# A routing step's list of tokens per slot: one-hot rows compared eight tiles at a time, the token number multiplied in on GpSimd

## The reference

```
x = x + layernorm(attention(layernorm(x)))        # 16 query heads, one key/value head, causal
x = x + layernorm(ffn(layernorm(x)))

def ffn(x):                                       # T = 4096 tokens
    probs = softmax(x @ router.T)                 # 8 experts
    top_v, top_i = top_k(probs, 2); top_v /= sum(top_v)
    out = sum over a token's two experts e of top_v * expert_e(x)      # 352 wide, silu-gated
    return out + sigmoid(x @ shared_gate.T) * shared_expert(x)          # 1408 wide, silu-gated
```

## Time and profile before

| | us |
|---|---|
| median of 3 runs | 2149.88 |
| lowest and highest of them | 2144.54, 2150.34 |
| the profiled execution, its own time | 2153.74 |
| its span, first to last instruction | 2152.0 |
| mean granted TensorE clock, share of full | 0.943 |
| PE busy, share of the span | 92% |
| DVE busy | 52% |
| ACT busy | 36% |
| POOL busy | 22% |

### The profile page before, as it was taken

How to read it: one execution, slowest core, us unless ns; L and a number is a source line. 1 busy time by engine, 2 the same in 40 slices (tenths; PEclk the granted TensorE clock), 3 DMA queues, 4 the chain that set the end, 5 groups by cost and what they waited for, 6 DMA issues and landing times. The chain is left out here.

```text
span 2152.0 us, 34973 instructions
## 1 busy us (share of the span) xinstructions
PE 1973.5 (92%) x11932; PEld 1568.8 (73%) x11932; DVE 1129.8 (52%) x2478; ACT 781.6 (36%) x1576; POOL 478.2 (22%) x1087
## 2 busy tenths in 40 slices
PE   5989999999999743899999999999999999999995
PEld 3665656656565422799999999978888888888884
DVE  4556656666565328677777657643433324333243
ACT  3445545455453410466666546432111111111111
POOL 1223324234241320211111112001113021130212
PEclk9799999999999765899999989999999999999998
DMA  5144353442533132566666657632123020230202
GB/s 173 51 114 127 117 174 106 147 143 109 176 98 126 50 113 95 195 237 236 235 235 235 240 188 268 243 113 69 37 81 118 19 97 31 86 117 19 97 24 94
DMA packets 114453, 281.47 MB, mean 131 GB/s; under 512 B 11680, under 2 KB 26272, under 8 KB 105024
## 3 DMA queue, kind: packets, MB, share of 16 engines
q1 hardware_dynamic: 103328, 244.18, 32.9%
q0 software_dynamic: 11040, 36.18, 5.0%
HBM read 198.79 MB, written 78.12 MB: 129 GB/s over the span
## 5 line engine op out<-in xcount | busy, mean ns | idle before, releaser
L1257 PE MATMUL ex_bank<-ex_xT,ex_gu 128*128 128x256 f32 (+12 forms) x2808 | 358.0, 284 | 1.0 <-DVE ex_xT L1421 1.0
L1257 PEld LDWEIGHTS ex_bank<-ex_xT,ex_gu 128*128 128x128 f32 (+1 forms) x2808 | 344.1, 185 | 4.9 <-issue 1.4
L1289 DVE TENSOR_TENSOR sh_silu<-sh_silu,sh_bank 128x512 f32<-128x512 f32 x88 | 60.6, 688 | 457.4 <-ACT sh_silu L1282 451.1
L1282 ACT ACTIVATE sh_silu<-sh_bank 128x512 f32<-128x512 f32 x88 | 52.6, 598 | 591.4 <-PE sh_bank L1257 546.1
L1257 PE MATMUL sh_bank<-sh_xT,sh_gate 128*128 128x512 f32 x1056 | 256.2, 392 | 5.2 <-DVE sh_dn L1704 5.2
L677 DVE TENSOR_REDUCE at_nmax<-at_bank 128x1 fp32r<-128x384 f32 (+3 forms) x512 | 222.6, 476 | 61.2 <-PE at_bank L438 60.7
L1269 PE MATMUL sh_bank<-sh_dn,sh_act 128*128 128x512 f32 x1056 | 254.3, 390 | 0.0
L1257 PE MATMUL sh_bank<-sh_xT,sh_up 128*128 128x512 f32 x1056 | 253.7, 389 | 0.0
L1257 PEld LDWEIGHTS sh_bank<-sh_xT,sh_gate 128*128 128x128 f32 x1056 | 199.8, 189 | 47.3 <-issue 5.6
L869 ACT ACTIVATE at_PT<-at_bank 128x512 f32<-128x512 f32 (+1 forms) x384 | 184.2, 506 | 125.7 <-PE at_bank L451 101.0
L1269 PEld LDWEIGHTS sh_bank<-sh_dn,sh_act 128*128 128x128 f32 x1056 | 197.6, 188 | 43.7 <-DVE sh_act L1298 2.9
(11 more groups left out here) (228 smaller groups left out, 2653.8 us busy)
## 6 DMA issues: line engine op xcount, KB each, us to landing
ex_gu_in<-gu_in SPq DMA_DIRECT2D x39, 1408.0 KB
at_Qs<-q_dram SPq DMA_DIRECT2D x96, 256.0 KB, 4.0
ex_dn_in<-dn_in SPq DMA_DIRECT2D x39, 512.0 KB
ys<-sh_yk SPq DMA_DIRECT2D x35, 512.0 KB, 2.9
q_dram<-at_q_h SPq DMA_DIRECT2D x64, 256.0 KB, 3.2
xnT<-at_xT SPq DMA_DIRECT2D x16, 1024.0 KB, 5.0
sh_xT<-xnT SPq DMA_DIRECT2D x16, 1024.0 KB
at_x_in<-x_in SPq DMA_DIRECT2D x8, 1024.0 KB, 5.1
```

The source lines that it names most:

```text
L1257: last = self.nc.tensor.matmul(self.gate_up_ps[c % 2][which][0:m, 0:w], cols(i, k), self.xT[j][:, k, 0:w], start=(step == 0), stop=(step = ...
L1282: nc.scalar.activation(silu[c % 2][0:m, 0:w], gate_up_ps[c % 2][0][0:m, 0:w], ACT.Silu).then_inc(s["silu_ready"], 1)
L1289: nc.vector.tensor_tensor(silu[c % 2][0:m, 0:w], silu[c % 2][0:m, 0:w], gate_up_ps[c % 2][1][0:m, 0:w], ALU.mult).then_inc(s["product"], 1)
```

## The change

The one-hot rows of lanes are made eight tiles at a time as well, by one tensor_tensor compare of 128x1024 elements, without the token's number. The number is multiplied into the columns' side instead, by a tensor_tensor of 128x592 on GpSimd, from `column_hot` into a new tile `column_token`, which is what PE reads. All three tiles now have two buffers, used in turn by the PARTS = 8 parts (m) of eight picks. DVE signals `column_ready` behind each column compare, GpSimd `token_ready` behind each product. PE waits once for each part, for both its sides, and signals `used` once for each part. DVE waits before the column compare of part m for the product of part m - 2, and before the lane compare for the matmuls of part m - 2; GpSimd waits for these too, before it writes `column_token`.

```diff
-        lane_hot = [sb(f"lane_hot{k}", [P, P], F32R) for k in range(4)]
-        column_hot = sb("column_hot", [P, 2, NTT, SC], F32R)
+        PART = NTT // 4
+        PARTS = 2 * NTT // PART
+        lane_hot = [sb(f"lane_hot{k}", [P, PART, P], F32R) for k in range(2)]
+        column_hot = [sb(f"column_hot{k}", [P, PART, SC]) for k in range(2)]
+        column_token = [sb(f"column_token{k}", [P, PART, SC], F32R) for k in range(2)]
...
         def _(pool):
...
+            for m in range(PARTS):
+                t = m * PART % NTT
+                pool.wait_ge(column_ready, m + 1)
+                if m >= 2:
+                    pool.wait_ge(used, m - 1)
+                nc.gpsimd.tensor_tensor(column_token[m % 2][:], column_hot[m % 2][:],
+                                        token_no[:, t:t + PART].unsqueeze(2).to_broadcast([P, PART, SC]),
+                                        ALU.mult).then_inc(token_ready, 1)
...
         def _(pe):
...
-            for n in range(2 * NTT):
-                pe.wait_ge(hot, n + 1)
-                last = nc.tensor.matmul(inverse_ps[:, 0:SC], lane_hot[n % 4][:],
-                                        column_hot[:, n // NTT, n % NTT, :],
-                                        start=(n == 0), stop=(n == 2 * NTT - 1))
+            for m in range(PARTS):
+                pe.wait_ge(hot, m + 1)
+                pe.wait_ge(token_ready, m + 1)
+                for t in range(PART):
+                    last = nc.tensor.matmul(inverse_ps[:, 0:SC], lane_hot[m % 2][:, t, :], column_token[m % 2][:, t, :],
+                                            start=(m == t == 0), stop=(m == PARTS - 1 and t == PART - 1))
                 last.then_inc(used, 1)
...
         def _(dve):
...
-            for n in range(2 * NTT):
-                k, t = divmod(n, NTT)
-                if t % PART == 0:
-                    nc.vector.tensor_tensor(column_hot[:, k, t:t + PART, :],
-                                            column_no[:].unsqueeze(1).to_broadcast([P, PART, SC]),
-                                            digit_f[:, 0, k, t:t + PART].unsqueeze(2).to_broadcast([P, PART, SC]),
-                                            ALU.is_equal)
-                if n >= 4:
-                    dve.wait_ge(used, n - 3)
-                nc.vector.tensor_scalar(lane_hot[n % 4][:], lane_no[:], digit_f[:, 1, k, t:t + 1],
-                                        token_no[:, t:t + 1], ALU.is_equal, ALU.mult).then_inc(hot, 1)
-            dve.wait_ge(used, 2 * NTT)
+            for m in range(PARTS):
+                k, t = divmod(m * PART, NTT)
+                if m >= 2:
+                    dve.wait_ge(token_ready, m - 1)
+                nc.vector.tensor_tensor(column_hot[m % 2][:], column_no[:].unsqueeze(1).to_broadcast([P, PART, SC]),
+                                        digit_f[:, 0, k, t:t + PART].unsqueeze(2).to_broadcast([P, PART, SC]),
+                                        ALU.is_equal).then_inc(column_ready, 1)
+                if m >= 2:
+                    dve.wait_ge(used, m - 1)
+                nc.vector.tensor_tensor(lane_hot[m % 2][:], lane_no[:].unsqueeze(1).to_broadcast([P, PART, P]),
+                                        digit_f[:, 1, k, t:t + PART].unsqueeze(2).to_broadcast([P, PART, P]),
+                                        ALU.is_equal).then_inc(hot, 1)
+            dve.wait_ge(used, PARTS)
```

More of the change, by code:

```diff
@@ L1068, in build_routing @@
         own, expert_ready = sem("own"), sem("expert_ready")
-        PART = NTT // 4
+        column_ready, token_ready = sem("column_ready"), sem("token_ready")
         block = ctx.enter_context(nc.Block())
```

## The result

The changed kernel takes 2156.16 us at the median of 20 runs (2148.6 to 2159.31), the kernel before 2149.93 us in 20 runs beside them (2140.05 to 2154.74). The ratio is 1.0024 with a 95% interval of 1.0013 to 1.0035: slower by 0.24%, with an interval that reaches a little past 0.3%. The prediction had 2154.6 us and 0.22%. Its mechanism holds line by line in the trace. Its main sum does not: it made the list 4.7 us longer, and the trace shows 2.1 us.

A forecast was written before the change was run, and what follows sets the result against it. DVE was taken to pace the list. Eight parts in turns at 3.13 us, 25.0 us, plus the last burst of 2.04 put the cast 4.7 us later: 2149.9 + 4.7 = 2154.6 us, range 2146 to 2161.

The forecast's parts named there:

- Its mechanism: In the list's loop, DVE compares with two SBUF inputs and POOL's product take turns instead of overlapping.
- Its main sum: List loop: 3.13 us a part in turns, 25.0 us for eight; with the last burst, the cast comes 4.7 us later.
- What bounds, and what passes through: DVE paces the 22.51 us list stretch; everything behind is a chain, so its gain or delay reaches the kernel's end.
- The turns: In the list's loop, DVE's compares and POOL's product on SBUF run one after the other, 3.13 us a part.
- rival (a): In the list's loop, turns do not apply or cost little: 1.83 us a part, 5.3 us earlier, 2144.6 us; chance 0.12.
- Rows 8 to 10: Trace pairs near 11, 1551 and 177 us where POOL and DVE tensor_tensors on SBUF took turns, in both directions.
- DVE's terms: In each list part: column compare 0.69 us of pace, lane compare 1.22 us, pace 1.14; about 0.06 less taking over.
- The product: POOL's 592-element multiply in each list part: 1.45 us alone, in turns say 1.36 us.
- Rival (b): POOL's product is slower for its repeated operand: 4.1 us on top, 8.8 in all, 2158.7 us; chance 0.20.
- PE's bursts: Eight matmuls per list part, 0.23 us apart, 2.04 us a burst; only the last lies on the path.

The follow-up runs named there:

- experiments 2 and 8: Changed kernel with DVE's constant lane and column numbers read from PSUM, run twice: ratio to the kernel before 0.9979 both times, medians 2145.97 and 2145.6 us.
- experiment 2: Changed kernel with DVE's compares reading the constant lane and column numbers from PSUM, first run: 2145.97 us, ratio 0.9979 to the kernel before.
- experiment 4: Changed kernel with token numbers laid out 74 times each, so GpSimd's product reads a plain operand: ratio 1.0030 to the kernel before.
- experiments 2 to 4 and 8: Changed kernel with constants in PSUM (0.9979, twice), product on DVE (1.0019), or a plain operand for GpSimd's product (1.0030); ratios to the kernel before.
- the control: The kernel before, unchanged, run and profiled as if it were a variant: ratio 1.0004 (0.9989 to 1.0020).
- experiment 6: The kernel before with 16 lane tiles and PE's matmuls in bursts of eight, DVE's work unchanged: ratio 1.0005 (0.9989 to 1.0022).

## Why the prediction was right

**What bounds, and what passes through:** right. DVE set the pace before, the chain behind the list kept its distances, and a shorter list (experiments 2 and 8) shortened the kernel.

**The turns:** right, and this decided the sign. By lengths alone the list would have been 5.3 us shorter, which was rival (a). With GpSimd out of DVE's way it was 5.7 us shorter (experiment 2); as written it is 2.1 us longer. Rows 8 to 10 of before, three pairs among thousands of instructions, were enough to see it. The rule of the Trainium skill, "SBUF — State Buffer", section "Who interferes with whom", names two SBUF inputs on DVE as the condition; experiment 2 tests that and agrees, with 1.74 us against 0.76 for the same compare. The prediction left open who goes first when both wait. The loop leaves one such place in a part, behind the lane compare, since the next product needs the next column compare: there the waiting product went ahead of the column compare in all seven parts that have one to follow.

**DVE's terms:** right. The lane compare was put at 1.22 us and takes 1.21; its pace at 1.14, measured 1.13; taking over from POOL at 0.63 (0.69 less 0.06), measured 0.63.

**The product: this term was mis-sized,** and with it the sum. "1.17 + 80 x 0.00213 = 1.34, behind another product 1.39, on POOL: say 1.36" came from 512-element rows with two full operands. Measured are 1.03, so a part takes 2.80 us and not 3.13, and eight take 2.6 us less. Experiment 4 shows that the repeated operand is the reason (1.30 us with a plain one). Rival (b) had this very feature with the opposite sign: it asked what the repeats might cost on top, "It cannot be less than nothing". It can: a repeated operand is cheaper than a full one, and the bound from below was wrongly excluded.

**PE's bursts:** 1.90 us, 2.04 predicted, the spacing 0.21 us rather than 0.23. Together with smaller roundings this makes 24.6 us of list against 27.2 predicted.

**The time:** 2154.6 predicted, 2156.16 measured, and the agreement is better than the sum deserved. The list accounts for 2.1 us, 0.10%. The two series of runs give 1.0024 and 1.0020, 5.2 and 4.3 us; their intervals begin at 0.13% and 0.08%. So 2 to 3 us are not accounted for, and that they made up for the list's shortfall of 2.6 us is luck. The four profiles of each kernel put them neither in the list nor behind it. Their means put 2.0 us ahead of it: the list begins at 835.5 us before and at 837.5 after. That lies in the attention stage, which the change doesn't touch, for the routing takes 30.6 us up to the list in all eight; and the starts spread over 9 and 7 us, so it may be chance. Against chance speaks that all six series of runs with the changed loop (the two of the changed kernel, experiments 2 to 4 and 8) lie above what their lists, and in experiment 4 the layout, account for, by 0.8 to 3.1 us. But the control lies 0.9 us above as well, experiment 6 is 0.4 us below, its interval allows 3 us, and several series share their runs of before. Whether it is a real cost somewhere or scatter stays open.

## What to carry to other kernels

Before a product is moved from DVE to GpSimd, count the SBUF inputs of what DVE does meanwhile. With two on DVE's side the engines took turns here, and the move cost more (24.6 us of list) than doing the same product on DVE (23.6). If one of DVE's inputs is a constant, try it in PSUM: that alone made the same change worth having (16.8 us of list, against 22.5 before the change). And where busy time in a profile is high and lengths of one line fall into two groups (776 and 1742 ns), compare the ends of instructions across engines, since the second group may be waiting, as it was here.

## What was not expected of the hardware

- GpSimd's tensor_tensor of 128x592 with one operand repeated 74 times took 1.18 us beside compares that did not hold it up (experiment 2); from rows of two full operands 1.45 us had been worked out. In turns it ended 1.03 us behind the lane compare, and 1.30 us with a plain operand (experiment 4). Why the repeats make it cheaper, no run shows.
- Where a product and a column compare both waited for the lane compare to end, the product, begun first, went first, seven times of seven. Near 11 us of the kernel before it was otherwise: the GpSimd instruction of the earlier trace rows, begun at 11.43 behind the DVE one below, waited for that one and then for the next as well, which began 0.32 us later than GpSimd's.

```profile
11.42 0.41 DVE L660 TENSOR_TENSOR at_wvk<-at_x_res,at_wvk 128x256 fp32r<-128x256 f32 x1
```

- The clock's rise behind the first expert matmul varied from 3.16 to 4.88 us in four profiles of one kernel, and the start of the list by 9 us (831.9 to 840.7): one profile of each kernel would have put the change anywhere between a gain and a loss.
